# An attention layer with a gated side network: residual sums, weight loads and low-part loads in another order

## The reference

```
x: (8, 256, 512)                       # 2048 tokens of 512
xn  = layernorm(x)
s   = attention(xn)                    # 128 heads of width 4, 64 shared rope columns
                                       # softmax over 256 keys, then @ Wo
g   = silu(ffn(xn))                    # ffn(x) = q2( silu(q1(x)) * q3(x) )
                                       # q(x) = x @ tile(wq, 4).T + 0.5 * (x @ A.T) @ B.T
out = x + s * g
```

## Time and profile before

| what | value |
|---|---|
| median of three runs | 1886.9 us |
| the profiled execution | 1883.07 us |
| its span, first to last instruction | 1881.1 us |
| mean granted clock of PE, share of full | 0.994 |
| PE busy | 1846.7 us (98%) |
| PEld, DVE, ACT, POOL busy | 1473.5, 1358.9, 1427.1, 1462.3 us |
| HBM read, written | 61.26 MB, 35.65 MB |

### The profile page before, as it was taken

One profiled execution on the slowest core, in us unless ns is written; L12 is line 12 of the kernel. 1 busy time (PEld: TensorE's weight loads), 2 busy tenths in 40 slices (PEclk: granted clock), 3 DMA queues, 4 the chain that ended last, 5 costly groups with the idle time before them and its releaser, 6 DMA issues.

```text
span 1881.1 us, 41460 instructions
## 1 busy us (share of the span) xinstructions
PE 1846.7 (98%) x12538; PEld 1473.5 (78%) x12538; DVE 1358.9 (72%) x1449; ACT 1427.1 (76%) x1954; POOL 1462.3 (78%) x1416
## 2 busy tenths in 40 slices
PE   8999999999999999999999999999999999999998
PEld 7777888888888888788878888887888788766676
DVE  8667777777777777777777777777777777677655
ACT  5577888888888888888888888888888888653222
POOL 5348889898989898989899898989898989215442
PEclk9999999999999999999999999999999999999999
DMA  8744444454545454545445444545454545665542
GB/s 247 241 95 111 105 108 110 105 111 103 116 99 118 98 121 96 118 99 121 102 105 110 106 110 105 112 103 117 97 120 97 119 96 111 150 177 155 164 143 68
DMA packets 186551, 225.23 MB, mean 120 GB/s; under 512 B 59726, under 2 KB 113774, under 8 KB 186478
## 3 DMA queue, kind: packets, MB, share of 16 engines
q1 hardware_dynamic: 178496, 221.30, 50.5%
q10 hardware_dynamic: 8006, 3.30, 0.7%
HBM read 61.26 MB, written 35.65 MB: 52 GB/s over the span
## 4 chain that ended last, share of the span: by engine, by line
PE 80%; DMA 5%; SPq 4%; issue 3%; DVE 2%; POOL 1%; ACT 1%; POOLq 0%; DVEq 0%; ACTq 0%
PE st L1156 23%; PE pj L1190 18%; PE ob L1190 17%; PE sx L1169 12%; PE ob L1122 6%; DMA w_stage<-in_Wq_rope 2%; DMA num<-o_scratch 1%; DMA x_raw_h<-o_scratch 1%; POOL num L1557 1%; SPq L755 1%; DMA slot<-kc 1%; DVE pw L1057 1%; SPq L751 1%; SPq L1375 0%; DVE mx L1064 0%
## 5 line engine op out<-in xcount | busy, mean ns | idle before, releaser
L866 POOL TENSOR_TENSOR pw<-pf,pw 128x1024 f16<-128x1024 f32 x354 | 763.4, 2170 | 122.1 <-ACT pw L1044 81.9
L1064 DVE TENSOR_REDUCE mx<-sx 128x4 fp32r<-128x1024 f32 x512 | 626.7, 1224 | 304.7 <-PE sx L1169 299.8
L1035 ACT ACTIVATE pf<-st 128x1024 f32<-128x1024 f32 x472 | 453.5, 1010 | 2.8
L1156 PE MATMUL st<-slot,k 128*128 128x512 f32 x1024 | 409.0, 399 | 1.4 <-issue 1.4
L1156 PE MATMUL st<-slot,krlh 128*128 128x512 f32 x1024 | 402.3, 393 | 0.0
L1044 ACT ACTIVATE pw<-pf 128x1024 f16<-128x1024 f32 x354 | 360.9, 1052 | 11.9
L1169 PEld LDWEIGHTS sx<-k,slot 88*128 88x128 f32 x2048 | 312.5, 189 | 66.2 <-DMA slot<-kc 7.7
L1169 PE MATMUL sx<-k,slot 88*128 88x256 f32 x2048 | 332.2, 284 | 10.6 <-DMA slot<-kc 4.8
L1073 DVE TENSOR_TENSOR slot<-pj,slot 64x512 fp32r<-64x512 f32 x256 | 176.4, 689 | 100.1 <-ACT slot L966 95.4
L1156 PEld LDWEIGHTS st<-slot,k 128*128 128x128 f32 x1024 | 192.8, 188 | 55.5 <-issue 2.7
L1156 PEld LDWEIGHTS st<-slot,krlh 128*128 128x128 f32 x1024 | 193.2, 189 | 37.1
(11 more groups left out here) (244 smaller groups left out, 2642.5 us busy)
## 6 DMA issues: line engine op xcount, KB each, us to landing
slot<-slot SPq DMA_DIRECT2D x256, 256.0 KB, 3.0
k<-kc SPq DMA_DIRECT2D x256, 128.0 KB
w_stage<-in_Wq_rope SPq DMA_DIRECT2D x64, 256.0 KB, 4.4
o_scratch<-o_sb SPq DMA_DIRECT2D x256, 64.0 KB
c_scratch<-stage SPq DMA_DIRECT2D x32, 256.0 KB, 3.0
c_in<-c_scratch SPq DMA_DIRECT2D x128, 64.0 KB, 1.9
k<-kc SPq DMA_DIRECT2D x128, 48.0 KB
k<-kx SPq DMA_DIRECT2D x128, 48.0 KB
```

The source lines that it names most:

```text
L866: nc.gpsimd.tensor_tensor(pw[:, s, kt, 1], pf[:, 2 * odd + kt], pw[:, s, kt, 0], ALU.subtract).then_inc(lo_done[kt][odd], 1)
L1035: nc.scalar.activation(dst, st[:, kt], ACT.Exp, scale=SCALE).then_inc(exp_done, 1)
L1064: nc.vector.tensor_reduce(mx[:, p, lo:lo + 4], sx[:, :, :].rearrange("p a (b k) -> p (a b) k", b=2), axis=AX.X, op=ALU.max).then_inc(red_d ...
L1156: last = nc.tensor.matmul(st[:, kt, h, :].rearrange("p (e n) -> p e n", e=PH), kk, q[:, s, :, h, :], start=(n == 0), stop=(n == 1))
```

## The change

It has three parts, and two that follow from them.

First, in `pool_rest` the sums of parts 6 and 7 of the next chunk stand ahead of the residual addition of tile 2 instead of tile 1.

Second, ACT issues the three loads of w2 (128, 128 and 88 rows of 2 KB) at k = 8, 9 and 10, one each, instead of all at k = 11. The first pair of the small b2 loads goes from k = 11 to k = 12; the second stays at 13.

Third, the last four low parts (n = 4 to 7) of chunk 0 are no longer loaded at k = 16 (three of them) and k = 18 (the fourth, into a tile used twice): all four are loaded at k = 17, behind SP's wait for the row of maxima to land (`mrow_in`) and ahead of `load_den(1)`, each into a tile of its own. The fourth tile is a piece of `hid`; SP waits there for the scores of step 12, and DVE's product of hidden tile 8 in chunk 0 waits until the eight sums are done.

With these go two moves on DVE: the low parts `sl` of chunks 2 and 3 are taken in the ends of steps 12 and 14 instead of inside step 16 ahead of the maxima, and the low part of the first half of Wo (`weight_o_lo(dve, 0)`) behind the reciprocal at the end of step 16 instead of ahead of the maxima.

```diff
--- before.py
+++ after.py
@@ -1384,15 +1384,15 @@
         if n < KD:
             return den[:, n, :], part_loaded[0], KD * c + KD - 1
         if c == 0:
-            tile = (0, 1, 2, 0)[n - KD]
-            return (x_tile, hh[:, 1, :].bitcast(F32), hh[:, 2, :].bitcast(F32))[tile], part_loaded[1 + tile], int(n == 2 * KD - 1)
+            i = n - KD
+            return (x_tile, hh[:, 1, :].bitcast(F32), hh[:, 2, :].bitcast(F32), hid[:, 2, 0, :])[i], part_loaded[1 + i], 0
         i = n % 2
-        return (x_tile, spare_tile[:, :])[i], part_loaded[1 + 3 * i], (0 if i else 2) + 2 * (c - 1) + (n - KD) // 2
+        return (x_tile, spare_tile[:, :])[i], part_loaded[1 + 3 * i], 1 + 2 * (c - 1) + (n - KD) // 2
 
     def load_num_part(sp, c, n):
         tile, loaded, _ = num_part(c, n)
         if c == 0 and n == 2 * KD - 1:
-            sp.wait_ge(num_done, KD + 1)
+            sp.wait_ge(at_sems.st_done, 2 * projected(12))
         if c and n >= KD + 2:
             sp.wait_ge(num_done, c * 2 * KD + n - 1)
         kt, row = n % KD, NV + 2 * HD * (n // KD)
@@ -1418,14 +1418,13 @@
             for r in range(NR):
                 act.dma_start(a2[0:FR[r], r, :, 0:RANK],
                              a2T.rearrange("(j p) n -> p j n", j=4)[128 * r:128 * r + FR[r], :, :]).then_inc(a2_loaded, 16)
-        if k == 11:
-            for r in range(NR):
-                act.dma_start(w2_raw[r][0:FR[r]],
-                             blocks(w2qT[128 * r:128 * r + FR[r], :])).then_inc(w2_loaded, 16)
-        if k in (11, 13):
+        if k in (8, 9, 10):
+            r = k - 8
+            act.dma_start(w2_raw[r][0:FR[r]], blocks(w2qT[128 * r:128 * r + FR[r], :])).then_inc(w2_loaded, 16)
+        if k in (12, 13):
             act.wait_ge(ab2_zero, 2)
             for j in range(2):
-                row = 32 * (j + k - 11)
+                row = 32 * (j + 2 * (k - 12))
                 act.dma_start(b2_raw[row:row + 3 * RANK], blocks(b2T).unsqueeze(0).broadcast_to([3, RANK, 4, 128])).then_inc(b2_loaded, 16)
 
     def sync_tail(sp, k):
@@ -1458,11 +1457,7 @@
         if k == 16:
             sp.wait_ge(at_sems.proj_done, projected(15))
             load_num(sp, 0)
-            for n in range(KD + 1):
-                load_num_part(sp, 0, n)
-            for landed in at_sems.ct_in:
-                sp.wait_ge(landed, 64 * NT)
-            for n in (KD + 1, KD + 2):
+            for n in range(KD):
                 load_num_part(sp, 0, n)
             for row in (0, 32):
                 sp.dma_start(lora[64 + row:64 + row + LR, :].bitcast(F32), lora[row:row + LR, :].bitcast(F32)).then_inc(lora_copied, 16)
@@ -1470,6 +1465,10 @@
             sp.wait_ge(recip, 1)
             store_recip(sp, 0)
             sp.wait_ge(at_sems.mrow_in[1], 16 * NT)
+            for landed in at_sems.ct_in:
+                sp.wait_ge(landed, 64 * NT)
+            for n in range(KD, 2 * KD):
+                load_num_part(sp, 0, n)
             for q in range(2):
                 sp.wait_ge(at_sems.o_stored[q], 32 * (NT - 2))
             load_den(sp, 1)
@@ -1477,7 +1476,6 @@
             sp.wait_ge(num_done, KD)
             sp.wait_ge(r_stored, 16)
             spread_den(sp, 0)
-            load_num_part(sp, 0, 2 * KD - 1)
         if k == 19:
             sp.wait_ge(recip, 2)
             store_recip(sp, 1)
@@ -1567,7 +1565,7 @@
                 if c + 1 < NC:
                     if i == 0:
                         pool.wait_ge(hl_done, (c + 1) * NR)
-                    for n in (range(KD + 2), (KD + 2, KD + 3), (), ())[i]:
+                    for n in (range(KD + 2), (), (KD + 2, KD + 3), ())[i]:
                         summed(c + 1, n)
                 if ending(c) and i == NI - 1:
                     break
@@ -1685,21 +1683,25 @@
         nc.vector.tensor_tensor(wol[:, j:j + 2, :], wo_raw[:, j:j + 2, :], woh[:, j:j + 2, :],
                                 ALU.subtract).then_inc(wo_lo, 1)
 
+    def sums_lo(dve, chunks):
+        for c in chunks:
+            cs = slice(c * CH, (c + 1) * CH)
+            dve.wait_ge(sh_done, c + 1)
+            nc.vector.tensor_tensor(sl[:, cs], s_raw[:, cs], sh[:, cs], ALU.subtract).then_inc(sl_done, 1)
+
     def vector_tail(dve, k, waiting=False):
 
 
         if waiting:
-            if k in (12, 16):
-                for c in (0, 1) if k == 12 else (2, 3):
-                    cs = slice(c * CH, (c + 1) * CH)
-                    dve.wait_ge(sh_done, c + 1)
-                    nc.vector.tensor_tensor(sl[:, cs], s_raw[:, cs], sh[:, cs], ALU.subtract).then_inc(sl_done, 1)
-            if k == 16:
-                weight_o_lo(dve, 0)
+            if k == 12:
+                sums_lo(dve, (0, 1))
             return
         if k == 16:
             dve.wait_ge(den_loaded, 16)
             nc.vector.reciprocal(den1[0][:, :], den1[0][:, :]).then_inc(recip, 1)
+            weight_o_lo(dve, 0)
+        if k in (12, 14):
+            sums_lo(dve, (k // 2 - 4,))
         if k in (11, 14, 17):
             i = k // 3 - 3
             cs = slice(256 * i, 256 * i + 256)
@@ -1774,6 +1776,8 @@
                 dve.wait_ge(up_done, c * MT + m + 1)
                 if m == 0:
                     wait(dve, zmm_done, c)
+                if starting(c) and m == 8:
+                    dve.wait_ge(num_done, 2 * KD)
                 product = nc.vector.tensor_tensor(hid[0:n, r, j, :], up[m % 4][0:n, :], gate[0:n, m % 2, :], ALU.mult)
                 if r == 2:
                     lo = 32 * j
```

## The result

| what | before | changed |
|---|---|---|
| median of three runs | 1886.9 us | 1874.74 us (1872.38 to 1875.09) |
| ratio, 95% interval | | 0.9929 [0.9907, 0.9952] |
| profiled execution, its span | 1883.07, 1881.1 us | 1872.38, 1870.5 us |
| mean granted clock | 0.994 | 0.998 |

The forecast was 1874.1 us, in a range of 1867 to 1882.5.

A forecast was written before the change was run, and what follows sets the result against it. Outside the full-clock middle, PE's waits (7.4 us for res, 2.0 for a content load, the drain's) and the slow clock behind them bound the kernel. 9.7 + 1.6 + 1.5 = 12.8 us off 1886.9 gave 1874.1, range 1867 to 1882.5.

The forecast's parts named there:

- 9.7 forecast: Chunk boundaries: three PE waits for res (7.41 us) and 4.8 us of slow stretches go, less 1.0 and 1.5 us.
- a landing at 1745.42: First boundary: store of tile 1 estimated to land two transfers (1.36 us) behind store 0, freeing the product of tile 3.
- against 4.8: Chunk boundaries: slow stretches at the lower clock behind the three waits go, 3 x 1.6 = 4.8 us.
- The 1.0 us of waits that should have come back: Second and third boundaries: PE arrives earlier against POOL's and DVE's chains, so 0.3 and 0.7 us of wait return.
- The 1.5 us for DVE's sums beside POOL: Start of the next chunks: DVE's block sums slow beside POOL's longer run, 0.5 us taken off for each of three chunks.
- A block sum over 1.4 us: Sign that the forecast is wrong: DVE's block sums take more than 1.4 us.
- 1.6 forecast: Steps 11 and 12: earlier w2 loads shorten PE's 2.0 us wait for a content load by 1.6 us.
- less than 0.5 at step 12: Sign that the forecast is right: PE's wait at step 12 is under 0.5 us.
- +1.5 forecast: Drain: the maxima wait and its slow stretch go and later transfers limit the gain; 1.5 us taken, ends +5.6 and -2.9.
- what is late next is the load of `den_1`: Drain: four loads, 2.5 us of issues, precede den_1, which lands up to 1 us later; hid starts 0.2 to 2.4 us earlier.
- Rival 3: Drain: four loads make den_1 late, PE waits 1.3 us plus 1.6 at lower clock, 2.9 lost; 1878.5 us; chance 0.08.
- the 1.6 us that the forecast adds to each wait: Chunk boundaries: after each wait PE runs some eight matmuls at 1.2 GHz, 8 x 0.20 = 1.6 us lost.

The follow-up runs named there:

- 11.0 alone: The kernel before with only the sums of parts 6 and 7 put behind the residual addition of tile 1: 1876.79 us, ratio 0.9944.
- nothing alone (0.9993): The changed kernel with the POOL reordering and the w2 load moves taken back, leaving the low-part loads and DVE moves: 1886.73 us, ratio 0.9993.
- the run with both edits: The changed kernel with the four low-part loads behind den_1 and the next o_sb store, and POOL's normalisations of parts 0 and 1 earlier: 1871.26 us, ratio 0.9925.
- `den_1` first: The changed kernel with the load of den_1 issued ahead of the four low-part loads, the o_sb store still behind all: 1872.27 us, ratio 0.9926.
- one boundary undone: The changed kernel with the old order of residual addition and sums 6 and 7 at the boundary from chunk 1 to 2 only: 1876.38 us, ratio 0.9951.
- second profile of the changed kernel: The changed kernel, unaltered, run once more on another chip: 1873.39 us, ratio 0.9932.
- part 2 alone: The kernel before with only the w2 loads at steps 8, 9 and 10 and the b2 loads moved: 1883.81 us, ratio 0.9975.

## Why the prediction was right, and where not

The number came out 0.6 us off, with two of its three terms off by more than that.

- **Part 1: 9.7 forecast, 10.3 in the profile, 11.0 alone.** The chain was read right: the store of tile 1 was what came last. The product of tile 3 was estimated to follow a landing at 1745.42; it started at 1745.26, and PE took it up at 1746.10 without a wait that the views show. PE gained 4.65, 3.58 and 3.96 us at the three boundaries, 12.19 in all; 7.43 of these were won by the first narrow matmuls, where the waits stood, and that leaves 4.76 for the slow stretches, against 4.8. The 1.0 us of waits that should have come back did not. The 1.5 us for DVE's sums beside POOL came out at 1.86: 1.06 were given back in chunk 1, 0.71 in chunk 2 and 0.09 in chunk 3, 1.0 of them as the three waits for `hid` in the list of the profile after. So 7.43 + 4.76 - 1.86 = 10.3. A block sum over 1.4 us, which the forecast had named as a sign that it is wrong, was there (1.84), but its cost had been taken off. The sum that took 1.84 us instead of 0.69 lost 1.15, nearly a whole POOL operation of 1.25 to 1.29; the Trainium skill, "SBUF — State Buffer", section "Who interferes with whom", has the later of two such instructions wait for the end of the other, and that row agrees, while the sums of 1.07 us lost 0.38.
- **Part 2: 1.6 forecast, 0.8 in the profile.** The content wait fell, as said. What the forecast left out is the row of maxima, which ACT sends by the same queue: it was issued 4.3 us behind the third w2 load, took 5.1 us to land (before 2.2), and PE waited 1.04 us for it; the forecast had asked for less than 0.5 at step 12. With that load a step earlier it lands in 1.9. Over the profiles, the content waits and waits for the row in steps 11 and 12 sum to 1.98, 2.97 and 3.17 us with the old place (mean 2.7) and to 0.2 to 3.1 with the new one (eight profiles, mean 1.5). So the part is worth about 1.2 us, with a spread larger than itself.
- **Part 3: +1.5 forecast, -1.3 in the profile, nothing alone (0.9993).** The first half was right: 1.70 us of wait and the slow stretch went, 3.2 to 3.3 us. The failed step is "what is late next is the load of `den_1`". Behind `den_1` in SP's program stands the second store of `o_sb`, which I did not follow; the forecast speaks only of the first, issued at 1690.84. That one did come 3.7 us earlier (1687.14), but PE was 4.6 earlier by then, and ACT's copy behind it waited 1.12 us instead of 0.25, so that 0.8 us of the gain were gone at the last `ob`. The second store cost more.

Of before, SP's issues behind the row of maxima, and ACT's copy into the half that the second store frees:

```profile
1694.80 0.62 SPq L1361 DMA_DIRECT2D den<-o_scratch  x1
1695.54 1.11 SPq L799 DMA_DIRECT2D o_scratch<-o_sb  x2
...
1702.65 0.39 ACT L1015 ACTIVATE o_sb<-ob 128x256 f32<-128x256 f32 x1 [2.05 <-PE ob L1122]
```

of after, with the four loads in front:

```profile
1690.17 0.63 SPq L1399 DMA_DIRECT2D x_raw_h<-o_scratch  x1
1690.85 1.25 SPq L1399 DMA_DIRECT2D hh<-o_scratch  x2
1692.14 0.60 SPq L1399 DMA_DIRECT2D hid<-o_scratch  x1
1692.84 0.56 SPq L1361 DMA_DIRECT2D den<-o_scratch  x1
1693.53 1.22 SPq L799 DMA_DIRECT2D o_scratch<-o_sb  x2
...
1701.53 0.38 ACT L1015 ACTIVATE o_sb<-ob 128x256 f32<-128x256 f32 x1 [4.73 <-DMA o_scratch<-o_sb]
```

and of the run with both edits, with the loads behind:

```profile
1692.18 0.62 SPq L1361 DMA_DIRECT2D den<-o_scratch  x1
1692.91 1.12 SPq L799 DMA_DIRECT2D o_scratch<-o_sb  x2
```

ACT had the data ready at 1685.96. SP starts issuing when the row of maxima has landed (the first line of each fence) and goes on without a pause. So the second store is issued 0.74 us behind that landing in the kernel before, 0.73 with the loads behind, and 3.36 in the profile after: the 2.6 us between are the four issues, the same 2.5 us that the forecast had put ahead of `den_1`. The rest is their data, 1 MB ahead of the store: from its issue to its last packet of 1 KB, in the packet records of the traces, it takes 7.57 us (to 1701.10), against 6.36 before (to 1701.90) and 6.46 with the loads behind (to 1699.37). (The chain of waits puts the issue of `den_1` down to the landing of the first store, at 1693.21; but that issue begins at 1692.84, right behind the four others, so it did not wait there.)

So PE was 4.6 us earlier at the scores behind the row (1690.25 against 1694.87) and the store's last packet only 0.8. Before, ACT's copy came 0.75 us behind that packet and had waited for PE; in the profile after it follows by 0.43 and waited for the store. By these two numbers the store had some 0.3 us to spare (estimate). PE lost 2.29 us to it, and 1.6 to the lower clock behind. Rival 3 had the four loads as the cause and a wait with the lower clock as their effect, but the wrong transfer behind them: `den_1` ahead of the loads gave nothing, and `den_1` itself came 0.6 us earlier than before (1698.87 against 1699.51). For this part it had -2.9 us, where -1.3 were found.

The ledger of the profiles is 0.8 + 10.3 + 0.8 - 1.3 = 10.6 us, the difference of the spans. The first 0.8 lies ahead of all parts. The ratios of the two sessions (0.9929 and 0.9932) say 12.8 to 13.4 us of 1886.9; the 2 us between are within what profiles differ by at 1600 us already, ahead of all edits: against the profile after, the one of before is 1.35 us later there, and those with `den_1` first and with one boundary undone 3.6 and 3.7 us. That the forecast hit the median to 0.6 us is in part luck: by the profile its three parts are 12.8 forecast and 9.8 found, and what fills the gap lies outside the parts. The wrong sign of part 3 (2.8 us) is the one error that counts. Part 1, with 10.3 us, isn't luck: its chain was read from the rows, and the runs with it alone and with one boundary undone bear it out.

## What to carry to other kernels

When loads are moved in a queue, follow every transfer behind them to its reader, not only the next one: a store that frees one of two buffers is easily the late one, and both the issues and the data put ahead of it count (here 2.6 and about 1.1 us). A chain view infers what a step waited for; the start of the step says whether it can be so. An addition that a store waits for belongs ahead of work that waits for a load on the same engine. A wait removed in a chain of transfers gains only up to the slack of the next one, so list those slacks first.

## What the runs showed of the hardware

- The length of a wait alone does not say whether the clock falls behind it. It fell behind 1.70 us (the 0.72 of the earlier trace rows), 1.91 us (the second boundary), 1.76 (0.57 in the four us from step 12 on with `den_1` first) and 2.03 (0.66 from 1702 to 1706 in the second profile of the changed kernel), and stayed at 1.00 behind 1.98 us at step 12 of the kernel before, 2.13 us at the first narrow matmul of chunk 0 in the kernel with one boundary undone and 2.48 us in the drain with part 2 alone. So the 1.6 us that the forecast adds to each wait need not come with it; at the three boundaries it did.
- A transfer of 8 KB, alone in 1.9 us, took 5.1 us behind a load of 176 KB in its own queue beside a 688 KB load in SP's, and 6.2 in the drain, where the traffic was at 244 GB/s.
